# A four-layer graph network on one core: second attention gathered by group, GINE sums started from the node values, gathers at most three groups ahead

## The reference, cut to what matters

```
L0: two-head attention over the edges (GATv2):  e = leaky(xl[src] + xr[dst]); alpha = softmax per dst of e.att
    out = mean over heads of segment_sum(xl[src] * alpha, dst) + h @ res_W + bias ...
L1: one-head attention: m = leaky(xl[src] + xr[dst] + edge_weight * We); logits = m @ att
    out = segment_sum(xl[src] * softmax per dst of logits); x + out, gelu, batch norm
L2: three times (GINE):  e = edge_attr @ W_lin + b_lin;  msg = relu(x[src] + e)
    h = x + segment_sum(msg, dst);  h = relu(h @ W1 + b1) @ W2 + b2;  x = relu(batchnorm(h))
L3: an MLP on [x[src], x[dst], edge_attr] per edge, segment_sum to dst, an MLP per node, layer norm
```

## Time and profile before

| | us |
|---|---|
| median of three runs | 4297.43 |
| profiled execution | 4296.55 |
| its span, first to last instruction | 4294.7 |

### The profile page before, as it was taken

The page is one execution under the profiler, slowest core; times in us unless marked ns, Lnnn a source line. Parts: engine busy times, 40 slices in busy tenths (PEclk is TensorE's granted clock), DMA queues, the critical chain, the costliest instruction groups (busy, mean ns, idle before and its releaser), DMA issues. The chain is left out here.

```text
span 4294.7 us, 91663 instructions
## 1 busy us (share of the span) xinstructions
PE 3433.3 (80%) x20700; PEld 2674.9 (62%) x20793; DVE 2652.6 (62%) x6184; ACT 1616.2 (38%) x3137; POOL 2562.0 (60%) x2650
## 2 busy tenths in 40 slices
PE   6999999977777775766656666666665999999996
PEld 3777777754555543555545555455554888888894
DVE  5888888875666664433344333443335888888885
ACT  3666666644555553111121111211114333333334
POOL 4555555536777766777757777577772444444430
PEclk7999999988999995555565655655557999999998
DMA  3333333322333322222222222222222333333330
GB/s 118 89 101 100 99 99 101 99 69 65 80 80 81 80 66 60 69 67 67 68 61 68 67 67 67 60 67 68 67 67 73 109 107 111 108 106 111 108 93 15
DMA packets 293250, 349.78 MB, mean 81 GB/s; under 512 B 63536, under 2 KB 236755, under 8 KB 292915
## 3 DMA queue, kind: packets, MB, share of 16 engines
q0 software_dynamic: 98528, 229.12, 19.7%
q1 hardware_dynamic: 140481, 92.05, 8.0%
q10 hardware_dynamic: 54162, 27.77, 2.2%
HBM read 332.61 MB, written 16.07 MB: 81 GB/s over the span
## 5 line engine op out<-in xcount | busy, mean ns | idle before, releaser
L988 POOL DMA_INDIRECT gath<-source_rows_narrow,gine_idx x1176 | 1145.3, 974 | 429.9 <-issue 357.8
L1036 DVE TENSOR_TENSOR vs<-psum,gath 128x512 f32<-128x512 f32 x366 | 253.1, 692 | 804.9 <-SPq L973 677.9
L1142 POOL DMA_INDIRECT gath<-source_rows,idx_all x416 | 430.6, 1035 | 508.1 <-DVE vs L1263 351.3
L1002 PE MATMUL psum<-gine_lin,ea 32*128 32x128 f32 x2928 | 285.9, 479 | 516.1 <-DVE vs L1036 487.0
L760 POOL DMA_INDIRECT gath<-source_rows,idx_all x488 | 465.2, 953 | 374.6 <-PE psum L807 259.6
L760 POOL DMA_INDIRECT gath<-source_rows_narrow,idx_all x488 | 464.6, 952 | 205.3 <-issue 137.2
L1002 PEld LDWEIGHTS psum<-gine_lin,ea 32*128 32x128 f32 x2928 | 182.1, 294 | 618.3 <-DVE vs L1036 554.8
L790 PE MATMUL psum<-lk,att_b 128*128 128x512 f32 x732 | 373.9, 617 | 112.5 <-DVE lk L885 111.8
L807 PEld LDWEIGHTS psum<-gath,pt 128*128 128x128 f32 x2928 | 365.4, 192 | 36.8 <-DVE zsum L918 1.8
L1011 PE MATMUL psum<-hot,pm 128*128 128x128 f32 x1488 | 372.3, 429 | 17.0 <-ACT pm L1066 16.1
L1066 ACT ACTIVATE pm<-vs 128x512 f32<-128x512 f32 x186 | 117.3, 630 | 690.9 <-DVE vs L1036 686.4
(11 more groups left out here) (242 smaller groups left out, 6131.9 us busy)
## 6 DMA issues: line engine op xcount, KB each, us to landing
rel<-rel_rows SPq DMA_DIRECT2D x244, 128.0 KB
ea<-in_edge_attr_tiles SPq DMA_DIRECT2D x416, 64.0 KB
ea<-in_edge_attr ACTq DMA_DIRECT2D x366, 64.0 KB
gath<-source_rows_narrow,gine_idx POOLq DMA_INDIRECT x1176, 2.5
gath<-source_rows,idx_all POOLq DMA_INDIRECT x904
rel<-quad_rel_rows SPq DMA_DIRECT2D x104, 128.0 KB
gath<-source_rows_narrow,idx_all POOLq DMA_INDIRECT x488
source_rows<-ACC SPq DMA_DIRECT2D x12, 512.0 KB, 2.9
```

Source lines behind the costliest of these rows:

```text
L988: pool.indirect_dma_start(out=ring[:, g % RING, j, :], out_offset=None, in_=table1, in_offset=bass.IndirectOffsetOnAxis(ap=gine_idx[:, g, ...
L1002: last = e.matmul(E[:, j, :], ea[rows, s, :], gine_lin[rows, layer, :], start=True, stop=True)
L1036: v.tensor_tensor(vs[:, s, :].rearrange("p (j d) -> p j d", j=SUBS), E, ring[:, bass.ds(slot, 1), :, :].rearrange("p a j d -> p (a j) d"), ...
L1142: pool.indirect_dma_start(out=gath[:, q % 4, j, :], out_offset=None, in_=table, in_offset=bass.IndirectOffsetOnAxis(ap=quad_idx[:, q, j:j ...
```

## The change

1. *Second attention by group* (`by_group`, only where heads == 1). GpSimd gathers each of the 98 groups once, into the ring of eight slots. Before the ninth and later groups it reads `group_end` of the group eight before and waits until ScalarE has taken all its items (`rows_taken`). After each group it waits for the landing of the group before and counts it in `rows_landed`. ScalarE gets a new step `take(i + 1)` behind the copy L820 of item i: it reads group and slot of item i + 1, waits for `rows_landed` and for the sum that used the target slot before, and copies 128 x 512 values out of the ring into one of four slots in the free half of `ACC` (`rows`). TensorE reads `rows` in the place of `gath` and waits for `rows_taken`.
2. *GINE accumulators.* VectorE fills `acc` with a copy of `XT` in the place of the memset; the seven adds L1572 and the waits on them (`gn_h`) go.
3. *Three groups ahead.* In `gine_edges`, GpSimd waits for the group three before (`AHEAD = 3`) and not for that eight before, and SyncE's `used` follows one group behind the landing and not four.
4. Semaphore counts are adapted, since the ring's semaphores now count one more round and `gathered` one less.

```diff
@@ -47,6 +47,7 @@
 RING = 8
+AHEAD = 3
@@ -706,6 +707,8 @@
         gathered = [sem(f"gathered{s}") for s in range(4)]
+        gi_gath = [sem(f"group_gathered{s}") for s in range(RING)]
+        rows_landed, rows_taken, slot_free = (sem(f"gat1_{k}") for k in ("rows_landed", "rows_taken", "slot_free"))
@@ -719,6 +722,8 @@
             w_in = [sem(f"{name}_w_in{s}") for s in range(2)] if with_weight else []
+            by_group = heads == 1
+            rows = ACC[:, NODE_BLOCKS * D:NODE_BLOCKS * D + 4 * GROUP_EDGES].rearrange("p (s j d) -> p s j d", s=4, j=SUBS) if by_group else gath
             cleared, hot_t_done, negs, g_ready, g_copied, v_ready, v_added, leaked, s_ready, s_masked, neg_max_new, max_step, max_done, p_ready, scl_ready, \
@@ -754,6 +759,25 @@
                 def _(pool):
+                    def report(g):
+                        pool.wait_ge(gi_gath[g % RING], 16 * SUBS * (g // RING + 1))
+                        pool.nop().then_inc(rows_landed, 1)
+
+                    if by_group:
+                        pool.wait_ge(gine_idx_in, 16)
+                        for g in range(GROUPS):
+                            if g >= RING:
+                                end = pool.value_load(group_end[0:1, g - RING:g - RING + 1], min_val=1, max_val=ITEMS)
+                                pool.wait_ge(rows_taken, end)
+                                pool.nop().then_inc(slot_free, 1)
+                            for j in range(SUBS):
+                                pool.indirect_dma_start(
+                                    out=ring[:, g % RING, j, :], out_offset=None, in_=dram,
+                                    in_offset=bass.IndirectOffsetOnAxis(ap=gine_idx[:, g, j:j + 1], axis=0)).then_inc(gi_gath[g % RING], 16)
+                            if g >= 1:
+                                report(g - 1)
+                        report(GROUPS - 1)
+                        return
                     for i in range(ITEMS):
@@ -765,11 +789,14 @@
-                        e.wait_ge(gathered[s4], 16 * SUBS * (turn4 + 1))
+                        if by_group:
+                            e.wait_ge(rows_taken, i + 1)
+                        else:
+                            e.wait_ge(gathered[s4], 16 * SUBS * (turn4 + 1))
                         for h in range(heads):
...
                             for j in range(SUBS):
-                                last = e.transpose(T[h][:, j * P:(j + 1) * P], gath[:, s4, j, h * D:(h + 1) * D], ident)
+                                last = e.transpose(T[h][:, j * P:(j + 1) * P], rows[:, s4, j, h * D:(h + 1) * D], ident)
                             last.then_inc(g_ready, 1)
@@ -804,7 +831,7 @@
                             for j in range(SUBS):
-                                last = e.matmul(O[h], pt[:, h, j, :], gath[:, s4, j, h * D:(h + 1) * D],
+                                last = e.matmul(O[h], pt[:, h, j, :], rows[:, s4, j, h * D:(h + 1) * D],
                                                 start=(j == 0), stop=(j == SUBS - 1))
@@ -818,6 +845,8 @@
                             a.activation(vs[:, h, :], T[h], ACT.Copy).then_inc(g_copied, 1)
+                        if by_group and not (isinstance(i, int) and i == ITEMS - 1):
+                            take(i + 1, (s4 + 1) % 4)
@@ -828,6 +857,17 @@
                             mask(i + 1, 1 - s, turn + s)
+
+                    def take(i, s4):
+                        _, (g, slot) = nc.values_load_multi_w_load_instructions(
+                            groups_blocks[0:1, bass.ds(i, 1), 0:2], engines=(mybir.EngineType.Activation,),
+                            min_val=0, max_val=GROUPS - 1)
+                        slot = nc.s_assert_within(slot, 0, RING - 1)
+                        a.wait_ge(rows_landed, g + 1)
+                        if not isinstance(i, int) or i >= 4:
+                            a.wait_ge(o_ready, before_h + i - 3)
+                        a.activation(rows[:, s4, :, :], ring[:, bass.ds(slot, 1), :, :].rearrange("p a j d -> p (a j) d"),
+                                     ACT.Copy).then_inc(rows_taken, 1)
@@ -845,6 +885,8 @@
                     mask(0, 0, number * PAIRS)
+                    if by_group:
+                        take(0, 0)
                     walk(a, front, back, mid, layer=number)
@@ -926,7 +968,6 @@
         gi_ea = [sem(f"gine_ea_in{s}") for s in range(2)]
-        gi_gath = [sem(f"gine_gathered{s}") for s in range(RING)]
         gi_landed, gi_free = sem("gine_landed"), sem("gine_free")
@@ -947,7 +988,7 @@
-                    return 16 * SUBS * (layer * -(-(GROUPS - slot) // RING) + round + 1)
+                    return 16 * SUBS * ((layer + 1) * -(-(GROUPS - slot) // RING) + round + 1)
@@ -971,19 +1012,18 @@
                         sp.nop().then_inc(gi_landed, 1)
-                        if not isinstance(g, int) or g >= 4:
-                            used(g - 4)
+                        if not isinstance(g, int) or g >= 1:
+                            used(g - 1)
                     by_group(sp, group)
-                    for g in range(GROUPS - 4, GROUPS):
-                        used(g)
+                    used(GROUPS - 1)
...
                     for g in range(GROUPS):
-                        if g >= RING:
-                            pool.wait_ge(gi_free, layer * GROUPS + g - RING + 1)
+                        if g >= AHEAD:
+                            pool.wait_ge(gi_free, layer * GROUPS + g - AHEAD + 1)
                         for j in range(SUBS):
@@ -1015,7 +1055,7 @@
                 def _(v):
-                    v.memset(acc, 0.0).then_inc(gi["cleared"], 1)
+                    v.tensor_copy(acc, XT[:, :]).then_inc(gi["cleared"], 1)
                     v.wait_ge(gi["cleared"], layer + 1)
@@ -1074,7 +1114,7 @@
             ea_before, rel_before = 16 * GINE_LAYERS * PAIRS, 16 * 2 * PAIRS
-            gathered_before = [16 * SUBS * 2 * -(-(ITEMS - m) // 4) for m in range(4)]
+            gathered_before = [16 * SUBS * -(-(ITEMS - m) // 4) for m in range(4)]
             cleared, hot_t_done, hot_done, counted, h1_ready, h1_added, turned, h1_done, h2_ready, h2_added, h2_done, o_ready, acc_step = (
@@ -1554,8 +1594,8 @@
-        gn_h, gn_mm1, gn_u, gn_mm2, gn_y, gn_stat, gn_normed, gn_turned, gn_rows, gn_stored = (sem(f"gine_node_{k}") for k in (
-            "h", "mm1", "u", "mm2", "y", "stat", "normed", "turned", "rows", "stored"))
+        gn_mm1, gn_u, gn_mm2, gn_y, gn_stat, gn_normed, gn_turned, gn_rows, gn_stored = (sem(f"gine_node_{k}") for k in (
+            "mm1", "u", "mm2", "y", "stat", "normed", "turned", "rows", "stored"))
@@ -1568,8 +1608,6 @@
                 def _(v):
-                    for c in range(CHUNKS):
-                        v.tensor_tensor(h[:, at(c)], h[:, at(c)], XT[:, at(c)], ALU.add).then_inc(gn_h, 1)
                     for c in range(CHUNKS):
@@ -1589,7 +1627,6 @@
                     def first(c):
-                        e.wait_ge(gn_h, base + c + 1)
                         if c >= 2:
@@ -1624,7 +1661,6 @@
-                    a.wait_ge(gn_h, base + CHUNKS)
                     hidden(0)
```

## The result

The changed kernel takes 4310.19 us in the median (4306.88 to 4311.14, 8 runs) beside 4297.3 for the kernel before on the same chip; the ratio is 1.0028, 95% interval 1.0019 to 1.0037. The forecast was 4283: 14 us less than before, where 13 more were measured. The time still lies inside the stated range of 4264 to 4314. The profiled execution has a span of 4308.9 us, 14.2 more than before.

The account below looks back on a forecast made before the run. GpSimd's gather issue was taken to bound the second attention and GINE layers. Terms: -11.7 (second attention), -4.2 (node additions), +1.8 (copy for memset), sum -14.1 us, giving 4283 us; range 4264 to 4314.

Parts of the forecast that it names:

- GpSimd paces: Second attention: GpSimd's gather issue sets the 5.05 us per item, with an arithmetic loop nearly as long beneath it.
- rival 2: Second attention not relieved: the 5.05 us are PE's and VectorE's own, fewer gathers bring nothing; 4295 us, chance 0.13.
- The loop underneath, 4.88: Second attention: VectorE's loop free of gathers takes 4.88 us an item, so the gain is at most 20 us.
- R = 1.40: Second attention: time from the start of ScalarE's L820 to its new copy, mostly register reads; forecast 1.40 us.
- ScalarE's loop, R + 3.56: Second attention: new loop through ScalarE's copy, exponential and PE's transposes and logits product; 4.96 us, rounded to 4.95.
- each step takes the larger: Second attention: VectorE's and ScalarE's loops share PE but are not added; gain 11.7 us.
- Rival 1: Second attention: ScalarE becomes the bound from R = 1.49 us; 4308 to 4322 us, chance 0.20.
- Start of the stage, hidden: Second attention's start: the first copy delays item 0's transposes some 2 us, hidden by VectorE clearing its accumulators.
- Node additions gone, -1.4 a layer: GINE node passes: dropping the seven adds lets ScalarE start 2.1 us sooner; gain 1.4 us a layer, 4.2 in all.
- the copy for the memset, +0.6: GINE layer start: VectorE's copy lengthens a GpSimd gather; loss 0.6 us a layer, 1.8 in all.
- Three groups ahead, 0: GINE layers: the cap of three groups costs 0, as SyncE frees groups with over 2 us left.
- rival 3: GINE: GpSimd's phase against VectorE shifts and lengthened gathers may vanish, 30 us less; 4253 us, chance 0.12.

Follow-up runs that it names:

- b_three: The kernel before with three of the four gathers of each second-attention item, a quarter of the rows left out: 4297.40 us, ratio 0.9993.
- early: The changed kernel with ScalarE's group and slot reads moved into its idle time and the copy two items ahead, after the mask: 4294.80 us, ratio 0.9987.
- gine_only: The kernel before with only the three GINE edits, its second attention unchanged: 4293.83 us, ratio 0.9992.
- gat_only: The changed kernel's second attention alone, with GINE layers and node passes of the kernel before: 4316.82 us, ratio 1.0048.
- early_dve: The kernel early with VectorE's block-number read moved from before the leaky step to after the item's comparison: 4259.71 us, ratio 0.9922.

## Why the prediction was wrong, step by step

1. **"GpSimd paces", second attention bound twice over: wrong, and the decisive step.** The gathers were 5.05 us apart because the items were. The sign was there in the earlier trace rows and was explained away: GpSimd's recurring waits on PE, about one a turn. b_three settles it: with a quarter of the gathers gone the period stays at 5.03. This was rival 2, and I gave it 0.13. But rival 2 alone would have given 4295; the loss that came on top is step 4.
2. **The loop underneath, 4.88: mis-sized.** It was summed from one item and one mean gap. The item shown held no turn of the loop: every fourth distance is 5.33, the other three 4.93 in the mean, the mean of the four 5.03. The turn thus makes 0.10 of the missing 0.15 us, the parts mixed from different items the rest. The 0.17 us by 117 items that the change was to free did not exist. A list of the logits products' starts shows this at sight.
3. **R = 1.40: right.** 1.43 us in the median and 1.45 in the mean measured (1.27 to 1.72 in single items). The clock ratio of 0.80 in the Trainium skill (Advanced Engine Details and Errata, Clock Domains) had given 1.37; the trace lies a little above both.
4. **ScalarE's loop, R + 3.56, and "each step takes the larger" of two loops: wrong in its second half.** ScalarE's own turn measures 4.92 in one item (L847 1300.41 to 1305.33; predicted 4.96), and with VectorE's read out of the way it gives 5.01. But with both present the period was 5.168, above either: the exponential's lateness passes through L826, L817, L884 and L799 into VectorE's addition, and the register read before the leaky step is then served behind it. So two loops that share an engine in a fixed order can add in part. Measured is that the period falls to 5.01 without VectorE's read there, and to 5.03 to 5.04 without either of ScalarE's two parts ahead of the exponential; the way from one engine to the next is read from the trace. Rival 1 named this place but put its price on R; the price came at the R that I had forecast.
5. **Start of the stage, hidden: mis-sized.** The first item is no later for it: from the stage's first gather to its first logits product pass 31.7 us before and after. The second is: from the first to the second logits product 6.30 us before, 8.01 after, 6.94 without reads, 6.30 in early. That is 1.7 us once; kernels with before's attention scatter from 6.3 to 6.7.
6. **Node additions gone, -1.4 a layer, and the copy for the memset, +0.6: both mis-sized, the sum right by luck.** The copy's rows answer to the earlier trace rows:

```profile
2206.42 1.83 DVE L1058 COPY ACC<-XT 128x3200 f32<-128x3200 f32 x1 [3.25 <-PEq L1608]
```

```profile
2207.02 2.04 POOL L1028 DMA_INDIRECT gath<-source_rows_narrow,gine_idx  x1 [34.80 <-POOLq L1608]
```

The gather is not done until 0.8 us after the copy's end and takes 2.04 instead of 0.95 us: 1.1, not 0.6; so in all three layers. The copy's length of 1.83 us was foreseen by a row, 1.9. An estimate by the Trainium skill (VectorE: DVE Perf Modes, Mode 2x_2P) was 1.7; the trace lies a little above it. The node pass, answering to the earlier trace rows:

```profile
2179.46 3.75 PE L1632 MATMUL psum<-ACC,gine_w 128*128 128x512 f32 x4 [0.83 <-PEq L988]
```

```profile
2181.54 0.69 ACT L1658 ACTIVATE ACC<-psum,gine_cols 128x512 f32<-128x512 f32 x1 [5.05 <-PE psum L1632]
...
2184.95 0.69 ACT L1662 ACTIVATE XT<-psum,gine_cols 128x512 f32<-128x512 f32 x1 [1.02 <-PE psum L1638]
```

ScalarE starts 2.7 us after the last addition of the layer (2178.84), before 4.55, so 1.85 sooner where 2.1 was forecast, but PE's first products still take 1.7 to 1.9 each. From the last addition to the normalisation the passes of the three layers take 17.21, 17.35, 16.72 us beside 17.46, 18.40, 18.04 before: 0.9 a layer, not 1.4. By these two parts the GINE edits should cost 0.7 us (3.3 lost, 2.6 gained), where I had put -2.4, and gine_only measures -3, interval -7 to 0. In the trace of after the 1173 other gathers of GINE take 6.3 us less in all than before (gine_only 6.9 less, but gat_only, with before's GINE code, also 2.7 less). Why is open; single layers scatter by 1 to 2 us between kernels with the same GINE code.
7. **Three groups ahead, 0: right** as far as these runs can tell. No shift of phase: not settled, by the shorter gathers of step 6; a shift worth rival 3's 30 us did not come.

The sum at its true sizes: no gain in the stage; by steps 4 and 5 +16 us in the profiled pair (14.1 over the 120 later distances and 1.7 at the start), +20 by gat_only's ratio; some -3 of GINE; +13 measured.

## What to carry to other kernels

Before pricing relief for an engine, list the starts of one instruction per item over two turns of the loop: the mean of these distances is the period, the sum over one item is not. An engine whose work per item equals the period may be following it; take a quarter of its work away to see. Work put ahead of an instruction that others wait for costs nothing as long as it fits into the room behind it, and only the sum counts: here the reads alone and the copy alone ahead of the exponential were free, both together cost 17 us (ratio 1.0028 beside 0.9987), and both were free again at another place. The gathers by group, worth nothing at first, belong to kernels 0.8% faster than before once another register read had left VectorE's loop (0.6 us in its place, 0.25 us off the period: 5.036 to 4.791).

## What the runs showed of the hardware that I had not expected

- Once in four items, at the turn of the loop that is unrolled by four, the distance is 0.4 us longer (5.33 beside 4.93), with TensorE idle 0.39 for "issue" before the V products (28 times in the 29 turns between 1000 and 1590 us of b_three). What in the turn takes the time was not looked at.
- A one-input fp32 copy on VectorE of 128x3200 takes 1.83 us, and a gather that starts inside it takes 2.04 us instead of 0.95 and ends 0.8 us after it (2206.42 + 1.83 = 2208.25; 2207.02 + 2.04 = 2209.06). The other layers' copies do the same (2.12 us where the gather took 1.06 before, and 2.05 where it took 0.95); the memset of 2.73 us did not lengthen one.
- VectorE's read of two registers between two dependent instructions costs 0.6 us: 1.34 us in the mean from addition to leaky step in after (1.16 to 1.67), 0.72 to 0.73 in early_dve, where it stands elsewhere.
